# Attention of a two-layer kernel: rounds in pairs of heads, outputs in groups of 256 queries, all products split

## The reference

```python
qs, ksem = heads of x @ wq_sem, x @ wk_sem          # 16 heads, 64 features
qg, kg = _rope(heads of x @ wq_geo), _rope(heads of x @ wk_geo)
v = (x @ wv).reshape(b, sl, 16, 128)
scores = g * qs.ksem / 8 + (1.0 - g) * qg.kg / 8     # g = sigmoid(gate_logit), one a head
attn = softmax(where(causal, scores, -1e9))
out = (attn @ v).reshape(b, sl, 16 * 128) @ wo
```

## Time and profile before

| | |
|---|---|
| median of three runs | 1967.28 us |
| profiled execution | 1968.04 us, its span 1966.4 us |
| TensorE busy | 1781.5 us, 91% |
| VectorE busy | 1106.4 us, 56% |
| ScalarE busy | 972.0 us, 49% |
| GpSimd busy | 802.1 us, 41% |
| attention, 460 to 1500 us | TensorE 999.7, VectorE 558.6, ScalarE 562.0, GpSimd 426.5 us of 1040 |

### The profile page before, as it was taken

How to read it: one execution, slowest core, us unless ns; L and a number is a source line. 1 busy time by engine, 2 the same in 40 slices (tenths; PEclk the granted TensorE clock), 3 DMA queues, 4 the chain that set the end, 5 groups by cost and what they waited for, 6 DMA issues and landing times. The chain is left out here.

```text
span 1966.4 us, 33208 instructions
## 1 busy us (share of the span) xinstructions
PE 1781.5 (91%) x9018; PEld 1315.6 (67%) x9018; DVE 1106.4 (56%) x2157; ACT 972.0 (49%) x2052; POOL 802.1 (41%) x788
## 2 busy tenths in 40 slices
PE   6399988439999999999999999999999999999998
PEld 2256656427777777777777777777776677677777
DVE  4799953695546455554645454555544333334467
ACT  4599923015555555555555455555554344444322
POOL 1489931333433444343434434443432233222354
PEclk9599999559999999999999999999999999999999
DMA  4753258200000000000000000000101999999623
GB/s 138 287 183 105 98 154 261 84 3 20 9 20 16 21 8 19 16 20 7 16 21 8 19 16 21 8 19 16 39 9 31 286 313 314 308 315 321 192 87 97
DMA packets 99216, 192.94 MB, mean 98 GB/s; under 512 B 15332, under 2 KB 59620, under 8 KB 96596
## 3 DMA queue, kind: packets, MB, share of 16 engines
q1 hardware_dynamic: 57684, 108.76, 18.0%
q0 software_dynamic: 17152, 47.67, 7.5%
q10 hardware_dynamic: 24336, 35.98, 5.5%
HBM read 140.84 MB, written 51.51 MB: 98 GB/s over the span
## 5 line engine op out<-in xcount | busy, mean ns | idle before, releaser
L1175 POOL TENSOR_TENSOR sw<-sw,rope_t 64x512 f32<-64x512 f32 x128 | 164.3, 1283 | 611.9 <-ACT sw L995 611.9
L1078 DVE TENSOR_TENSOR t<-ps,rope_t 128x512 f32<-128x512 f32 x128 | 88.5, 692 | 363.5 <-ACT sw L995 363.4
L890 PE MATMUL ps<-pt,v 128*128 128x512 f32 (+3 forms) x768 | 270.1, 495 | 19.8 <-DVE xr L1095 17.8
L987 ACT ACTIVATE pb<-ps,negmax 128x128 f32<-128x128 f32 (+7 forms) x256 | 191.1, 747 | 177.1 <-DVE negmax L1063 177.0
L1063 DVE TENSOR_REDUCE negmax<-ps 128x1 f32<-128x128 f32 (+7 forms) x256 | 191.9, 750 | 78.1 <-PE ps L849 76.1
L890 PEld LDWEIGHTS ps<-pt,v 128*128 128x128 f32 x768 | 139.1, 191 | 121.4 <-issue 79.5
L541 POOL DMA_DIRECT2D w2r<-in_w x148 | 77.5, 523 | 326.1 <-PE ps L590 306.3
L1178 POOL TENSOR_TENSOR t<-t,sw 64x512 f32<-64x512 f32 x128 | 179.1, 1399 | 33.6 <-POOL sw L1175 17.9
L883 PE MATMUL ps<-ident,pb 128*128 128x128 f32 x1152 | 171.3, 276 | 23.6 <-ACT pb L987 23.4
L974 ACT COPY pt<-ps 128x512 f32<-128x512 f32 (+3 forms) x256 | 130.1, 508 | 102.0 <-PE ps L883 94.5
L883 PEld LDWEIGHTS ps<-ident,pb 128*128 128x128 f32 x1152 | 133.8, 141 | 68.1 <-ACT pb L987 45.1
(11 more groups left out here) (198 smaller groups left out, 3677.2 us busy)
## 6 DMA issues: line engine op xcount, KB each, us to landing
w13r<-in_w SPq DMA_DIRECT2D x124, 352.0 KB, 6.0
w2r<-in_w POOLq DMA_DIRECT2D x148, 176.0 KB, 6.0
result<-yy ACTq DMA_DIRECT2D x148, 128.0 KB, 5.1
crow<-c_rows SPq DMA_DIRECT2D x32, 512.0 KB, 3.6
t<-sorted SPq DMA_DIRECT2D x124, 128.0 KB, 5.5
sorted<-zeros ACTq DMA_DIRECT2D x15, 1024.0 KB, 16.9
hc<-in_w SPq DMA_DIRECT2D x24, 352.0 KB, 5.3
wraw<-in_wqkv SPq DMA_DIRECT2D x16, 384.0 KB, 3.3
```

The source lines that it names most:

```text
L890: last = pe.matmul(ps[:, 6, c0:512], v[:, buf, j], pt[g][:, j, c0:512], start=j == 0, stop=j == 4 * g + 3)
L987: act.activation(pb[:, qt % 2, 0:cols], ps[:, bank:bank + 2, :].rearrange("p a n -> p (a n)")[:, 0:cols], ACT.Exp, bias=negmax[:, par, qn: ...
L1175: g.tensor_tensor(sw[64:128, p % 2, :], sw[64:128, p % 2, :], rope_t[64:128, 1, (p // 2) * 512:(p // 2 + 1) * 512], ALU.mult).then_inc(s_t ...
```

## The change

- A round is now one head of one batch in the order head 0 and 1 of batch 0, head 0 and 1 of batch 1, then the next pair of heads. The values of both heads of a pair are made together, in the first head's round, in steps 0, 1, 4 and 7 (four fillings of bank 7), not ahead of each round.
- The output is made in four groups of 256 queries: groups 0, 1, 2 in steps 2, 4, 6, group 3 in step 0 of the next round; each is projected one step later. The probabilities, values, value weights, outputs and `wo` are all split, and their products use `three`.
- ScalarE's copy of the transposed probabilities, now of all key tiles, is the rounded part (ahead of the next exponential, as the copy was). VectorE subtracts it from PSUM for the remainder, and so for values and outputs. Banks 4, 5, 6 and 7 come free when VectorE has subtracted.
- VectorE splits value weights once a pair, `wo` and query and key weights once a head, in steps 1 and 4.
- Memory: `xnT1` shares its place with the queries and keys; `w2r1` moves to memory that attention uses, so GpSimd waits for the end of attention before it loads the first second weights.

```diff
+            def values(m, b, fill):
+                pe.wait_ge(s_e7, fill - 1)
+                for a in range(2):
+                    t0 = b * SEQ + (2 * m + a) * P
+                    o = ps[:, 7, a * 2 * P:(a + 1) * 2 * P]
+                    for c in range(DC):
+                        last = three(pe, o, xnr[:, c, t0:t0 + P], xnl[:, c, t0:t0 + P], wvr[:, c], wvl[:, c], c == 0, c == DC - 1)
+                last.then_inc(s_b7, 1)
...
+                    w(pe, s_pl, CHUNKS * it + ci - 1)
                     for j in range(j0, j1):
                         last = pe.transpose(ps[:, 4 + ci % 2, (j - j0) * P:(j - j0 + 1) * P], pb[:, qt % 2, j * P:(j + 1) * P], ident[:])
...
+            def output(it, g, hh):
+                w(pe, s_e6, output_fill(it, g) - 1)
+                pe.wait_ge(s_pl, CHUNKS * it + (2, 4, 8, 12)[g])
+                hd = slice(hh * P, (hh + 1) * P)
+                for j in range(2 * g + 2):
+                    c0 = P if j == 2 * g + 1 else 0
+                    last = three(pe, ps[:, 6, c0:2 * P], vr[:, j, hd], vl[:, j, hd], ptr[g % 2][:, j, c0:2 * P], ptl[g % 2][:, j, c0:2 * P],
+                                 j == 0, j == 2 * g + 1)
+                last.then_inc(s_b6, 1)
+
+            def project_out(it, g, slot):
+                pe.wait_ge(s_e6, project_fill(it, g) - 1)
+                for a in range(2):
+                    sl = slice(a * P, (a + 1) * P)
+                    last = three(pe, ps[:, 6, a * D:(a + 1) * D], otr[:, sl], otl[:, sl], wor[:, slot], wol[:, slot], True, True)
+                last.then_inc(s_b6, 1)
...
+                    if qt == 0 and not first(it):
+                        if hh == 1:
+                            pe.wait_ge(s_e7, value_fill(pair, 3))
+                        output(it - 1, 3, 1 - hh)
+                    if qt == 1 and not first(it):
+                        project_out(it - 1, 3, 1 - hh)
+                    if qt in (2, 4, 6):
+                        output(it, qt // 2 - 1, hh)
+                    if qt in (3, 5, 7):
+                        project_out(it, qt // 2 - 1, hh)
+                    if qt in VALUE and hh == 0:
+                        values(VALUE[qt], b, value_fill(pair, VALUE[qt]))
+                    if qt in PIECE and not last:
+                        piece(p, next_b, 1 - hh, piece_fill(pair, hh, p))
...
+            def probs(it, qt):                                   # ScalarE
+                for ci, j0, j1 in chunks(qt):
+                    act.wait_ge(s_T, CHUNKS * it + ci + 1)
+                    act.copy(ptr[g % 2][:, j0:j1, cols], ps[:, 4 + ci % 2, 0:(j1 - j0) * P].rearrange("p (j q) -> p j q", q=P)).then_inc(s_pr, 1)
...
+                for ci, j0, j1 in chunks(qt):                    # VectorE
+                    dve.wait_ge(s_pr, CHUNKS * it + ci + 1)
+                    dve.tensor_tensor(ptl[g % 2][o], ps[:, 4 + ci % 2, 0:(j1 - j0) * P].rearrange("p (j q) -> p j q", q=P),
+                                      ptr[g % 2][o].bitcast(F32), ALU.subtract).then_inc(s_pl, 1)
...
                 for qt in range(8):                              # VectorE's order
                     if qt < 7 or not last:
+                        max_tile(it, qt + 1, hh)
+                    probs(it, qt)
+                    if qt == 0 and not first(it):
+                        rest(n0 - 1, 3, hh)
                     if qt in (4, 5, 7) and not last:
+                        rest(n0 + p, p, 1 - hh)
+                    if qt == 0 and not first(it):
+                        output(it - 1, 3)
+                    if qt == 1 and not first(it):
+                        add_out(it - 1, 3, prev_b, 1 - hh)
+                    if qt in (2, 4, 6):
+                        output(it, qt // 2 - 1)
+                    if qt in (3, 7):
+                        invert(it, qt // 7, hh)
+                    if qt in (3, 5, 7):
+                        add_out(it, qt // 2 - 1, b, hh)
+                    if qt in VALUE and hh == 0:
+                        values(VALUE[qt], 4 * pair + VALUE[qt] + 1)
+                    if qt in PIECE and not last:
                         turned(n0 + p, p)
+                    if qt == 1 and c == 2 and not last_pair(hp):
+                        split_qk(2 * hp + 2, 0)
+                    if qt == 1 and c == 3 and not last_pair(hp):
+                        split_qk(2 * hp + 3, 1)
+                        split_values(hp + 1)
+                    if qt == 4 and c == 3 and not last_pair(hp):
+                        split_wo(2 * hp + 2, 0)
+                    if qt == 4 and c == 0 and not first(it):
+                        split_wo(2 * hp + 1, 1)
...
             att_pool(g)
+            g.wait_ge(s_e6, ALL_OUTPUTS)
             experts_pool(g, R1, shared_splits(g))
```

More of the change, by code:

```diff
@@ L798, in build, with output_fill, project_fill, first_fill @@
         CHUNKS = 12
[L800 to L809, removed]
-        def heads_loop(eng, body):
[L813 to L819, removed]
+        def output_fill(it, g):
+            return 8 * it + 2 * g + 1
+        def project_fill(it, g):
+            return 8 * it + 2 * g + 2
+        V01, V23, Q0, K0, V45, Q1, K1_, V67 = range(8)
+        def first_fill(pair, n):
+            return 4 + 12 * pair + n + 1
+        def second_fill(pair, p):
+            return 4 + 12 * pair + 8 + p + 1
+        PIECE = {2: 0, 3: 1, 5: 2, 6: 3}
+        VALUE = {0: 0, 1: 1, 4: 2, 7: 3}
+        def piece_fill(pair, hh, p):
+            return second_fill(pair, p) if hh else first_fill(pair, (Q0, K0, Q1, K1_)[p])
+        def value_fill(pair, m):
+            return first_fill(pair, (V01, V23, V45, V67)[m])
+        ALL_OUTPUTS = 8 * ITS
+        ALL_BANK7 = 4 + 12 * (ITS // 2) - 4
+        def heads_loop(eng, body):
+            def four(hp, ends):
+                for c in range(4):
+                    body(hp, c, ends and c == 3)
+            four(0, False)
+            with eng.Fori(1, PAIRS_H - 1) as hp:
+                four(hp, False)
+            four(PAIRS_H - 1, True)
         def first(it):
             return isinstance(it, int) and it == 0
+        def last_pair(hp):
+            return isinstance(hp, int) and hp == PAIRS_H - 1
         def three(pe, out_ap, a_r, a_l, b_r, b_l, start, stop):
@@ L924, in att_pe, with body @@
             scores(0, 1, 0)
[L926 to L927 removed]
+            def body(hp, c, last):
+                it, pair = 4 * hp + c, 2 * hp + c // 2
+                b, hh = c // 2, c % 2
+                next_b = ((c + 1) % 4) // 2
                 for qt in range(8):
@@ L930, in body @@
                     if qt < 6:
-                        scores(it, qt + 2, b)
+                        scores(it, qt + 2, hh)
                     elif not last:
[L933 to L951, removed]
@@ L957, in att_pe @@
+                    if qt in PIECE and not last:
+                        p = PIECE[qt]
+                        if qt == 2 and next_b == 0:
+                            pe.wait_ge(s_ws, 2 * hp + c // 3 * 2 + (1 - hh) + 1)
+                        piece(p, next_b, 1 - hh, piece_fill(pair, hh, p))
             heads_loop(pe, body)
-            for part in range(2):
-                output1(ITS, 0, part)
-            for which, n in ((2, W2), (3, W3)):
-                project_out(which, use6(ITS, n))
+            output(ITS - 1, 3, 1)
@@ L1143, in body @@
-                    if qt == 6:
-                        add_out(1, b, use6(it, W1))
-                    if qt in (2, 3, 5, 6) and not last:
-                        p = {2: 0, 3: 1, 5: 2, 6: 3}[qt]
-                        turned(n0 + p, p)
-                    if qt in (2, 3) and not first(it):
-                        add_out(qt, 1 - b, use6(it, W2 if qt == 2 else W3))
-                    if qt == 5:
-                        add_out(0, b, use6(it, W0))
-                    if qt == 0 and b == 1 and not (isinstance(h, int) and h == HEADS - 1):
-                        dve.wait_ge(s_b7, use7(it - 1, 4))
-                        split(h + 1)
```

316 lines of the change are left out of this document (156 added, 160 removed).

## The result

The changed kernel takes 2021.36 us (median of four runs, 2011.48 to 2026.89) against 1968.05 beside it (four runs, 1965.22 to 1969.99): a ratio of 1.0267, interval 1.0223 to 1.031. It is slower, as forecast, but by 53 us and not by 10, and outside the range. Its profiled execution lasted 2019.35 us, span 2017.7.

What follows compares the result with a forecast made beforehand. TensorE's work sets the round now; after, no engine's sum but the order decides. Rounds +9, head +2.7, last round -2.5, tail -1.8, expert weights +2.3 make +9.7 on 1967.3: 1977 us, range 1925 to 2018.

Steps and rivals of the forecast that it cites:

- TensorE's work a round: TensorE's products in one attention round, starts added up part by part: from 32.0 to 30.5 us.
- the casts: ScalarE's casts to float32r, 617 ns against 587 for a copy, some five on the chain: 0.15 us a round.
- last round and tail: Last round without pieces, -2.5 us; from last output to last add, one projection in place of two, -1.8 us.
- start of round 0 and expert stage: Second head split and half-rate clock entering round 0, +2.7 us; later second expert weight loads, +2.3 us.
- the layout: Attention round followed, joint by joint: first head 34.95 us, second 31.28, mean 33.1, with weight splits 33.8.
- rival 2: TensorE's clock falls once a pair, in step 7 of the second head: +38 us, 2015 us; chance 0.10.
- Rival 1: Attention gaps stay as they are, TensorE's saving arrives: 32.2 us a round, 1922 us; chance 0.25, in full or half.
- the joint named against it: Step 7: bank 6 has one buffer, so the last output waits for the output add, behind two subtractions.
- max(3) behind the splits: Step 1: VectorE's weight splits stand ahead of step 3's maximum; 0.66 us a round come through.
- Rival 3: VectorE in order costs more, 0.06 us more at each of 16 joints: 35 us a round, 2008 us; chance 0.10.
- Rival 4: Weight loads bind TensorE's short float32r products: 7.6 us a round; chance 0.02.
- w2 term: Expert stage: four second-weight loads of 176 KB start only after attention, with DMA engines full: +2.3 us.

Runs made afterwards that it cites:

- k2: The change with its pairs written out, step 7's output add and ScalarE's exponential moved earlier, weight splits in step 0: 1916.34 us, 0.9791 of before.
- u0: The change with its eight pairs of heads written out and step 0's score products computed three times more: 1977.32 us, 1.0041 of before.
- a_unroll: The change with its eight pairs of heads written out, no loop: 1989.8 us, 1.0102 of before.
- c_warm: The change, loop kept, with step 0's score products computed three times more, overwriting: 1990.35 us, 1.0117 of before.
- k1_loop: The change with its loop, extra score products, step 7's output add and exponential earlier, splits in step 0: 1950.45 us, 0.9973 of before.
- u1: u0 with step 7's key remainder behind the output add and ScalarE's rounding of piece 2 behind the exponential: 1961.33 us, 0.9969 of before.
- u2: u0 with the weight splits moved from step 1 to step 0: 1959.56 us, 0.996 of before.

## Why the prediction was wrong

The sign was right, the size was not. By the prediction's steps:

| step | forecast | measured |
|---|---|---|
| TensorE's work a round | 30.5 us | 30.6 (k2) |
| key remainder in step 7 | 0.62 us | 0.82 in the mean |
| subtraction, 512 and 128 columns | 681, 281 ns | 682, 281 |
| cast of 512 columns from PSUM | 617 ns | 588 |
| VectorE a round | 25 us | 24.4 (747.74 / 1080 x 35.26) |
| a round, clock up and no jumps | 33.95 us (33.76 without the casts) | 33.74 (u0) |
| clock in attention | 1.00 | 0.96 |
| a round of the change | 33.95 us | 35.26 |
| waits of TensorE in attention | over 80 us | 105 |
| last round and tail | -4.3 us | -3.9 in u0, -0.9 in the change |
| start of round 0 and expert stage | +5.0 us | -0.8 and +3.5 |

The change's last round holds two more falls of the clock, at 1541.8 and 1565.7, which u0's does not. The half rate forecast for the start of round 0 came (the clock is 0.55 from 446 to 450 us, where it was 1.00).

**The step that failed** is the one in which the layout was taken for the round: "Clock 1.00 throughout attention", with rival 2 given 0.10. It came: 19 falls where the rival said 16, and up to 39 us of lost rate where it said 38. That the two sums agree is in part luck, since a fall costs 1.7 or 3.4 us here and not 2.4. Its place was half right. The rival named step 7 of a second head; half of the falls are behind a first head, where the last output waits 1.9 us for the value remainder, a joint that the layout has (it put 0.61 us on it) and that was never held against the clock. The earlier trace rows were read as waits "up to 1.2" that left the clock up. That rests on one wait, in the last round of the kernel before:

```profile
1512.52 1.09 PE L883 MATMUL ps<-ident,pb 128*128 128x128 f32 x8 [1.24 <-ACT pb L987]
```

All others of its attention are 0.7 us or less. What was missed is that the layout's own gaps lay outside what those rows can speak for: 1.2 and 1.4 us with 0.7 us of work between them in a second head's step 7, a pair like the one in a_unroll behind which the clock fell, and a longer one in a first head's. c_warm shows the cause: filling that gap gives back 31 us.

**What was not foreseen** is the jump. The change makes the loop's body twice as many rounds, and the sum has no term for that: a jump stands in it at nothing. The traces show instruction packets and stalls of 1.7 to 4.1 us together behind each jump back, which makes the fetching of code the likely cause. The price is 32 us by a_unroll, where a fall of the clock often follows the stall, 15 by k1_loop, where it rarely does. The two overlap: taking both away gives 44 us (1.0267 to 1.0041), not 63. With them gone the kernel takes 1977.3 us, the forecast of 1977, though that is in part luck, since u0 carries the extra products.

**Rival 1** (1922) was given 0.25 and did not come: the joint named against it is there, the last output behind the output add, and so is the layout's other one, max(3) behind the splits. Once u1 and u2 take them out it does come: 32.2 us a round was its number and 32.22 is k2's. **Rival 3** was not it: u0's rounds leave nothing for later joints. **Rival 4** neither: the products stand 0.12 apart with a load each.

**The w2 term** (+2.3) was not tried by itself. The trace shows the loads late, a wait of 5.01 us where there was one of 2.84 for tokens, and the stage from last add to the end took 444.7 us against 441.2. But it took 430 to 456 in the other runs, so the term can't be told from the rest.

## What to carry to other kernels

When a layout by hand makes a wait of TensorE longer than any that the trace shows at full clock, or puts two close together, half rate for some microseconds behind it belongs in the sum, not in a rival of one in ten. A change that lengthens a loop's body can have a price at each jump: look for waits for "issue" behind the jump, and for instruction packets in a window deep inside the loop, where a body that stays in place moves none. Packets over the whole run don't tell, since code written out moves them too. And where a layout names the joint that eats the gain, mend the joint before judging the idea: moving two groups of VectorE's work (and one rounding) was worth 61 us here with the rounds written out, more than the 53 that the change had cost.

## What the runs showed of the hardware

- TensorE's clock fell to 1.2 GHz behind some single waits of 1.75 to 1.9 us and behind some pairs of waits of 1.2 to 1.4 us with 0.9 us of work between, not behind all, stood there for 3.5 us of full work and rose again. In the rounds of k2, whose waits are up to 0.8 us, of the kernel before (up to 0.7, and one of 1.24 in the last) and of u0 (single ones of 1.3) it never fell. What decides between two equal waits was not found.
- Work that nobody needs can pay: 1.6 us of products a round in such a gap took 31 us off the kernel.
- The cost of a loop's jump depends on the body: from 620 to 1450 us 53 and 56 instruction packets and stalls of 1.7 to 4.1 us at a jump with the change's four rounds; 1 and 31 packets and some 0.5 us with four rounds of the kernel before; none with two. Where in between it begins was not tried.
- A round inside a loop took longer than the same one written out even away from the jump: 33.9 against 33.65 us in the kernel before.
- The same kernel, unchanged, took 1969 us on two chips and 1954 on a third; ratios were therefore taken against the runs beside each kernel.
